# Moving VectorE's patch-row copies and the first scaling of a norm in a fused two-convolution kernel

## The reference

```
x = x + L0(gn(x))        # attention-weighted depthwise 3x3 convolution, then 1x1
x = x + L1(gn(x))

def L1(x):
    hidden = einsum(w_hidden, x)                 # 32 -> 192 channels, 1x1
    hidden = depthwise 3x3 convolution of hidden
    q, k, v = split(hidden, 3)                   # 64 channels each
    out = irfft2(rfft2(q patches) * rfft2(k patches))      # patches of 8 x 8 pixels
    mu, var = mean and variance of out over the 64 channels of each pixel
    out_norm = (out - mu) / sqrt(var + 1e-5) * norm_w + norm_b
    return einsum(w_out, v * out_norm)           # 64 -> 32 channels, 1x1
```

## Time and profile before

| | before |
|---|---|
| median of 3 runs | 2357.64 us (2355.62 to 2362.33) |
| profiled execution | 2366.28 us, span 2364.4 us |
| PE, PEld busy | 95%, 61% of the span |
| DVE, ACT, POOL busy | 68%, 62%, 21% |
| length of a unit (first statistics at 1417.61 to the next unit's at 1474.04) | 56.43 us |

### The profile page before, as it was taken

One profiled execution on the slowest core, in us unless ns is written; L12 is line 12 of the kernel. 1 busy time (PEld: TensorE's weight loads), 2 busy tenths in 40 slices (PEclk: granted clock), 3 DMA queues, 4 the chain that ended last, 5 costly groups with the idle time before them and its releaser, 6 DMA issues.

```text
span 2364.4 us, 107028 instructions
## 1 busy us (share of the span) xinstructions
PE 2236.0 (95%) x48375; PEld 1443.6 (61%) x48375; DVE 1613.8 (68%) x4058; ACT 1454.2 (62%) x2629; POOL 486.3 (21%) x323
## 2 busy tenths in 40 slices
PE   7888888868999999999999999999999999999997
PEld 3333333346666666777676766667666666667664
DVE  5566766646777767767677667777777777777775
ACT  3456655566666666666666666666666666666662
POOL 1000000002222222222222222222222222222222
PEclk9889988978999999999999999999999999999999
DMA  7689888784333333333333333333333333333312
GB/s 140 168 212 234 226 204 219 214 200 103 75 76 76 76 76 76 79 81 76 84 73 79 76 84 80 84 81 84 76 84 76 83 78 76 76 76 76 76 43 50
DMA packets 60409, 248.63 MB, mean 105 GB/s; under 512 B 12393, under 2 KB 12658, under 8 KB 53810
## 3 DMA queue, kind: packets, MB, share of 16 engines
q1 hardware_dynamic: 59954, 241.78, 43.3%
HBM read 140.02 MB, written 101.72 MB: 102 GB/s over the span
## 4 chain that ended last, share of the span: by engine, by line
PE 84%; DVE 7%; ACT 4%; issue 4%; DMA 1%; SPq 0%; POOL 0%; POOLq 0%; ACTq 0%
PE bank L587 18%; PE bank L527 16%; PE bank L676 11%; PE bank L659 10%; PE bank L647 9%; PE bank L572 7%; PE bank L600 7%; PE bank L609 5%; DVE arena L1112 3%; ACT arena L865 2%; DVE arena L1132 1%; DVE arena L1125 1%; ACT arena L819 1%; DVE arena L1102 1%; ACT arena L724 1%
## 5 line engine op out<-in xcount | busy, mean ns | idle before, releaser
L456 POOL TENSOR_TENSOR arena<-arena 128x8 f32<-128x8 f32 x256 | 462.1, 1805 | 1357.6 <-DVE arena L1118 1352.6
L587 PE MATMUL bank<-arena 128*64 128x512 f16 x4608 | 689.9, 393 | 0.0
L810 ACT ACTIVATE arena<-bank 100x512 f32<-100x512 f32 x1024 | 606.6, 628 | 95.4 <-PE bank L572 75.1
L1197 DVE TENSOR_TENSOR arena<-bank,arena 128x512 f32<-128x512 f32 x512 | 337.2, 687 | 207.8 <-issue 174.0
L572 PEld LDWEIGHTS bank<-arena 128*36 128x36 f16 (+1 forms) x8192 | 330.5, 104 | 232.4 <-issue 23.5
L527 PE MATMUL bank<-arena 32*32 32x508 f32 (+1 forms) x9216 | 382.9, 649 | 55.4 <-issue 40.6
L572 PE MATMUL bank<-arena 128*36 128x128 f16 (+1 forms) x8192 | 390.5, 221 | 17.4 <-DVE arena L1102 11.5
L819 ACT ACTIVATE arena<-bank,arena 128x256 f32<-128x256 f32 x512 | 261.1, 560 | 119.9 <-PE bank L600 119.4
L852 ACT ACTIVATE arena<-bank 128x512 f32<-128x512 f32 x256 | 153.2, 598 | 265.7 <-PE bank L647 265.2
L1112 DVE BATCH_NORM_STATS2 arena<-arena 128x6 f32<-128x128 f32 x1024 | 221.7, 279 | 121.3 <-ACT arena L865 121.3
L647 PE MATMUL bank<-arena 100*32 100x128 f32 x8192 | 277.5, 274 | 5.2 <-issue 3.9
(11 more groups left out here) (112 smaller groups left out, 1605.1 us busy)
## 6 DMA issues: line engine op xcount, KB each, us to landing
arena<-xn_d SPq DMA_DIRECT2D x128, 536.2 KB, 4.8
xn_d<-arena SPq DMA_DIRECT2D x130, 260.0 KB, 4.5
x_d<-arena SPq DMA_DIRECT2D x64, 512.0 KB, 8.3
arena<-x_d SPq DMA_DIRECT2D x128, 256.0 KB, 4.2
out<-arena SPq DMA_DIRECT2D x128, 256.0 KB, 2.7
arena<-x_in SPq DMA_DIRECT2D x32, 544.0 KB, 9.6
arena<-x_in SPq DMA_DIRECT2D x32, 528.0 KB, 9.4
arena<-spectra_in SPq DMA_DIRECT2D x1, 384.0 KB
```

The lines of the kernel that those rows point to most:

```text
L456: pool.tensor_tensor(tiny["rstd"][:, slot], tiny["var_eps"][:, slot], powers, ALU.pow).then_inc(s_root, 1)
L587: mm = pe.matmul(v_banks[chunk % 3][64 * s:64 * s + 64, :], v_w[:, 64 * tap:64 * tap + 64], at(xs[u % 3], row * WP + 32 * k + dx, [32 * WP ...
L810: act.activation(h_rows[0:WIN, :, first:first + 4], ring[g % len(ring)][0:WIN, :].rearrange("p (i c) -> p c i", i=4), ACT.Copy).then_inc(s ...
L1197: dve.tensor_tensor(prod[:, first:first + 512].rearrange("p (a b x) -> p a b x", a=2, b=2), at(k_banks[m % 2], 256 * quad, [128, 2], [0, 2 ...
```

## The change

Two places of DVE's list are written anew; no instruction is added or removed, and the other engines' lists are untouched. In `front`, window 3 stands directly behind the statistics of piece 0 and ahead of centre 0; the statistics of piece 1 follow; scale 0 and centre 1 stand ahead of the statistics of piece 2 instead of behind them. In `spectral`, the three windows of the next unit stand behind the last of the sixteen products instead of behind products 8, 10 and 12.

```diff
@@ -1161,14 +1161,16 @@
                     for i in range(4):
                         low(NB - 1, i)
                     return
-                for p in range(3):
-                    pixel_stats(tail, p)
-                    variance(tail, p)
-                    if p == 1:
-                        centre(tail, 0)
+                pixel_stats(tail, 0)
+                variance(tail, 0)
                 windows()
+                centre(tail, 0)
+                pixel_stats(tail, 1)
+                variance(tail, 1)
                 scale(tail, 0)
                 centre(tail, 1)
+                pixel_stats(tail, 2)
+                variance(tail, 2)
                 scale(tail, 1)
                 windows()
                 for p in range(8):
@@ -1201,8 +1203,9 @@
                         gate(tail, 3, 1)
                     if n == 3 and tail is not None:
                         residual(tail, 3)
-                    if u < LAST and n in (8, 10, 12):
-                        window(u + 1, n // 2 - 4)
+                if u < LAST:
+                    for r in range(3):
+                        window(u + 1, r)
 
             dve.wait_ge(s_win_room, 3)
             for r in range(3):
```

## The result

| | before | after |
|---|---|---|
| median, 22 runs each | 2361.32 us | 2375.16 us (2363.57 to 2380.99) |
| ratio, 95% interval | 1 | 1.0052 (1.0039 to 1.0064) |
| span of the profiled execution | 2364.4 us | 2375.4 us |
| first statistics of the first front to those of the last (31 units) | 568.93 to 2320.86: 1751.9 us | 570.53 to 2332.27: 1761.7 us |

The change made the kernel slower by 0.52%, 12 us by the ratio. The two traces put nearly all of the difference, 9.8 of 11.0 us, between the first front and the last.

The account below looks back on a forecast made before the run. PE was taken to bound the kernel, busy 95% of the span. Per front, 0.38 us at the projection plus 0.05 for POOL, times 31, adds 13.3 to 2357.64: 2370.9 us, range 2361 to 2379 us.

Parts of the forecast that it names:

- What there was to win: At turn 0, PE's wait for scale 0 costs 0.41 us a front, 12.7 us over 31 fronts.
- Part 1 at zero: Three windows moved behind the products use DVE's idle time; cost zero, bounds -0.02 and +0.02 us a unit.
- The early wait: Window 3, ahead of centre 0, waits for hidden group 3; scale 0 and turn 0 come 0.15 us later.
- DVE's late second: After scale 0, the loop's first statistics start 1.01 us late, and DVE stays late until it has slack.
- Gate 2's slack: Ahead of gate 2, 0.55 us of DVE slack nearly absorbs its 0.63 us lateness over PE.
- The projection: The first projection's second half waits for late gate 1: 0.38 us later, including turn 0's 0.15.
- What would show it: Signs in a changed front's timeline, among them the first projection's load at 13.1 to 13.2 us instead of 12.72.
- the first rival: At the projection, the first half runs ahead and hides the wait; only turn 0's 0.15 us stays, 2362.3 us; chance 0.15.
- I would be wrong if L609 showed no wait for a gate: Sign at the first projection: PE or PEld should wait at L609 for gate 1; no size given.
- POOL: The root of piece 1 ends later and delays scale 1 by 0.05 us a front, 0.09 by the skill's rule.
- The size: Whole kernel: 0.43 us in each of 31 fronts, 13.3 us or 0.56% slower, 2370.9 us.

Follow-up runs that it names:

- e2_spectral_only: The kernel before with only the next unit's three windows moved behind the last product, the front as before; ratio 0.9997.
- e7_after_scale_gate1_first: The changed kernel with window 3 behind scale 0 instead of ahead of centre 0, and window 5 behind gate 1; ratio 0.9961.
- e4_gate1_first: The changed kernel with window 5 behind gate 1 instead of ahead of it; ratio 1.0006.
- the best version: The changed kernel with centre 0 behind the statistics of piece 1, scale 0 directly after it, then window 3; ratio 0.9955.

## Why the prediction was right, point by point

- **What there was to win.** The place was right, the size a little too large. 0.41 us was read from one front; over the 31, turn 0 starts 0.69 us behind its hidden group and 0.32 where it waits for nothing, so 0.37 us a front and 11.4 us in all were to be won. The version that wins it whole gained 11.2 us in the fronts. I also took the 31 waits of the earlier trace rows for the 31 fronts; 30 are, and the other is the last front's, which I put at nothing and which got 0.37 us shorter.
- **Part 1 at zero.** Right, 0.2 us in 31 units (e2_spectral_only). The products kept their end, as forecast: from the last of them to the first statistics it is 3.69 us in the median of both kernels. DVE's idle time in between went from 3.69 to 2.23 us, where I had "about 2.2". The front shown, with 2.64, is one whose products ended early, as happens in both kernels.
- **The early wait.** Window 3 was forecast 2.27 us after the first statistics, measured 2.26 in the front shown (2.21 to 2.30 over all). Scale 0 was forecast 0.15 us later; it is 0.15 in the front shown and 0.13 in the median.
- **DVE's late second.** Forecast 1.01 us at the statistics of piece 3, measured 1.02 (1.00 in the median). Gate 2's slack took it up, as forecast: no idle time is left there and the later gates are late by the same 0.36 us as PE (gate 3 at 20.06 instead of 19.70).
- **The projection.** The place and the sum were right, 0.38 forecast against 0.36, and so was the cause, as the runs with window 5 behind gate 1 show. The form was wrong in "What would show it", which has the projection's first load at 13.1 to 13.2 us. The first half's load started at 12.88, with turn 0's delay only, and only the second half waited for gate 1: the third of the four loads starts at 13.11, 0.05 us after gate 1 has ended, and these 0.05 us are the same in all 31 fronts. The row of the loads shows it: 0.42 us from the first to the last where there was 0.20.

```profile
1435.16 0.42 PEld L609 LDWEIGHTS bank<-arena 128*64 128x64 f32 x4
```

- That is the picture of the first rival, but not its price. The halves did run apart, and it saved nothing, since turn 2 stands behind both: the projection got 0.22 us longer instead of starting later. I had also written that I would be wrong if L609 showed no wait for a gate. It showed none to speak of: PE was busy with the first half all the while, and PEld was idle for 0.04 us only between the two halves' loads. That sign was badly chosen; the start-to-start distance of projection and turn 2 was the one to name.
- **POOL.** I had 0.05 us a front for scale 1 waiting for the root of piece 1, and 0.09 by the Trainium skill ("SBUF — State Buffer", "Who interferes with whom"). Both were too much: the root started at 4.57, was 2.02 us long and ended at 6.59, and scale 1 stood at 6.67, where DVE's own list put it. Without this term the sum is 0.38 us a front, 2369.4 us; with it 2370.9. The contention was there (2.02 instead of 1.64), its end just fell short of the step that needed it.
- **The size.** 0.56% was forecast, 0.52% measured. The sum of the terms measured in the trace is 0.36 us a front, 11.2 us, against 0.43 and 13.3. In absolute time the forecast stood on a median of three runs, 2357.64 us; over 22 runs before has 2361.32, and this makes up 3.7 of the 4.3 us between the forecast 2370.9 and the measured 2375.16.

What I did not see beforehand was in an experiment's expectation: that a centring placed at the start of a root delays it by half a microsecond. I had let DVE's order decide scale 0 alone and had put the root at its usual 1.64 us. I also wrote for e7_after_scale_gate1_first that turn 0 would lose 0.08 us to the late root; it came at the 4.68 I had written, but not for that reason, since scale 0 had ended 0.58 us before. The late root costs at the gates behind it. Turn 0 follows its hidden group by 0.32 us in both versions; the 4.68 against 4.64 is that group itself, which starts 0.05 us later in the two runs with centre 0 right behind the first statistics. No run isolates why.

## What to carry to other kernels

Before an instruction is moved up in an engine's list, look at its wait and not only at its length: what stands behind it pays for the time until the wait is met, and here one 0.48 us copy held a microsecond of work that PE needed. An idle microsecond put into a busy stretch stays until that engine's next slack, so go through every hand-over between the two places, not just the first. And when the gain of a reordering comes in at half, look for an instruction that is now placed beside another engine's start.

## What the runs showed of the hardware

- **A root on POOL is held by a centring or scaling on VectorE that had started before it.** These take two inputs from SBUF, and so does the root. Where nothing holds it, it takes 1.64 us. Started 0.04 us after centre 0, which ran 0.65 us more, it took 2.15; started at 1426.85 with scale 0 running until 1427.38, 0.53 us more, it took 2.02 (row below, from the changed kernel). In both cases the length is 1.64 plus the time the VectorE instruction still had to run, less 0.14 or 0.15. The Trainium skill ("SBUF — State Buffer", "Who interferes with whom") says that the later of two such instructions is blocked until the first is done; the trace agrees for the root, except that 0.14 us of what the VectorE instruction still had to run do not show in its length. It does not show the other direction: centre 0 of before starts 0.90 us after the root of piece 0, while that still runs, and takes its usual 0.69 us.

```profile
1426.85 2.02 POOL L456 TENSOR_TENSOR arena<-arena 128x8 f32<-128x8 f32 x1 [1.69 <-DVE arena L1118]
```

- **The window copy holds the root too, the gate does not.** In the kernel before, the root of piece 3 starts 0.16 us after gate 0, which takes one input from a bank and still runs for 0.52 us; it takes 1.63 us. The root of piece 4 starts 0.16 us after window 5, a copy within SBUF that still runs for 0.41 us, and takes 1.90, again 1.64 plus the rest less 0.15. With window 5 behind gate 1 (e4_gate1_first) it takes 1.63. POOL's two roots and the copy, before:

```profile
1425.58 1.63 POOL L456 TENSOR_TENSOR arena<-arena 128x8 f32<-128x8 f32 x1 [1.09 <-DVE arena L1118]
1428.65 1.90 POOL L456 TENSOR_TENSOR arena<-arena 128x8 f32<-128x8 f32 x1 [1.43 <-DVE arena L1118]
...
1428.49 0.57 DVE L1102 COPY arena<-arena 128x1600 f16<-128x1600 f16 x1
```

One root does not fit: the 2.23 us of the earlier trace rows, which starts with 0.30 us of scale 0 left and centre 1 close behind it. Two VectorE instructions in a row hold it for 0.59 us, more than the rest of the first and less than that of both.

- **Two matmul groups that write different halves of a bank's partitions run beside one another, and a wait of the second does not hold the first.** With gate 1 in time the four matmuls of the projection (two for each half) take 1.02 to 1.03 us from first to last, and in before they start in pairs, the two of a pair 0.005 us apart; with gate 1 late, 1.25, and the first half's start has turn 0's delay only.
- **VectorE takes up the next instruction before the last has ended**: 0.60 us from start to start of instructions that are 0.69 long, but 0.79 from the centring to the scaling of the same piece when they stand side by side, since the scaling waits for the centring and starts 0.10 us after its end. Before has one such pair ahead of the statistics of piece 3, at piece 1, and the best version one at piece 0; those statistics start at 6.76 and 6.77 us, so in this comparison the pair at piece 0 cost nothing more.
